# Layer norm over the heads of a decoder block: its mean folded into two weights, its Newton steps moved from VectorE to GpSimd

## The chip, the cores and the metric

The kernel runs on one core of a Trainium2 chip. Its time is the device time of one execution, in microseconds (us), given as the median of several runs. Five engines work beside each other, each through its own queue, strictly in the order of that queue: TensorE (PE), ScalarE (ACT), VectorE (DVE), GpSimd (POOL) and SyncE (SP, which only issues transfers). They wait for each other by semaphores.

## The reference, cut to what matters

Two decoder layers run over x and a context of 32 x 64 x 128 each. The first layer is: causal attention with 16 heads of 8, a cross attention, and a feed-forward part with fp4 rounding. Only the cross attention is touched. Its queries and keys are projected, and then each head (8 numbers) of each token is normed:

```python
def _layernorm(x, g, b):
    mu = jnp.mean(x, axis=-1, keepdims=True)
    var = jnp.mean(jnp.square(x - mu), axis=-1, keepdims=True)
    return (x - mu) * jax.lax.rsqrt(var + LN_EPS) * g + b
# q = _layernorm(heads of x @ Wq), k = _layernorm(heads of ctx @ Wk), LN_EPS = 1e-5
```

Then follow scores, softmax, the mix of values, a projection, the sum with x, and a norm over all 128 numbers of a token.

## The kernel before

The 2048 tokens are cut into four chunks of 512 (4 tiles of 128). Two chunks, the streams s0 and s1, run at a time, so the body of the loop runs twice; these are pass 1 and pass 2. Each engine's program for one stream is a Python generator (`network(h)`), and `weave` interleaves the programs of s0 and s1 by the numbers in `ORDER`, turn by turn. What stands in an engine's queue is thus fixed when the kernel is built: an instruction whose input is late holds up all behind it, of the other stream too.

A stream's way through the first attention and into the second, with the names used below:

- `attention_tiles` works on tiles t = 0 to 3 of a stream: scores (PE L494), row maximum and subtraction (DVE L1114, L1119), exponential (ACT L899), transposes (PE L479) and their copies (ACT L879), mix (PE L540), division (DVE L1129, L1132, into `heads`), transpose (PE L524), its copy (ACT L890), projection (PE L506), sum with x (DVE L1084), mean and variance (DVE L1087, L1090), reciprocal root of the variance (POOL L1512 adds epsilon, POOL L1515 raises to -0.5, into `rs`), and the normed x (DVE L1095).
- The keys of the second attention are projected early, in PSUM bank 1 (PE L551 from `cT`). This is norm j = 1, "k" below. The queries (PE L551 from `xT`, bank 0) come when x is there, with the values behind them (PE L465). This is norm j = 0, "q".
- `heads_norm` on DVE norms them, 64 heads of 8 per partition: `centre` sums each head (L1184), divides by 8 (L1187) and subtracts (L1190); ACT squares the result (`square_heads`, L863); `invert` sums the squares (L1195), adds epsilon (L1198), makes a first guess of the reciprocal root by an integer shift and subtraction (L1202, L1205) and begins three Newton steps of three instructions each (L1170, L1173, L1176); `scale` ends them and multiplies (L1214).
- PE turns the result (`turn_heads`, L564), ACT applies gain and bias (L869) and spreads queries (L850) or keys (L857, four instructions) for the scores. `take_values` (ACT L838) copies the values, and ACT L828 copies the turned x.
- `residual` (POOL L1531) adds a bias row to x for the sum of the second attention.

Ahead of the loop PE turns the fp4 weights (L809, L811), ACT copies them (L1027 to L1029), and SP issues all loads.

## Time and profile before

| | |
|---|---|
| median of 3 runs | 902.3 us (901.3 to 907.78) |
| span of the profiled execution | 900.6 us |
| busy: PE / DVE / ACT / POOL | 716.8 / 561.2 / 364.6 / 97.5 us |
| instructions: PE / DVE / ACT / POOL | 5017 / 1492 / 592 / 226 |
| chain that ended last: PE / DVE / ACT / POOL | 64% / 19% / 10% / 1% of the span |

The span goes from the first to the last instruction of one profiled execution; the median is of other executions, and lies 1.7 us above it. The profile counts one fp32 matmul as two records (the 128x128 projection L506 appears 96 times for 48 projections).

### The profile page before, as it was taken

How to read it: one execution, taken by the hardware profiler on the slowest of the kernel's cores; microseconds unless marked ns; L12 is line 12 of the kernel's file. 1: busy time of each engine (PE TensorE's matmuls, PEld its weight loads, DVE VectorE, ACT ScalarE, POOL GpSimd, SP SyncE). 2: the span in 40 equal slices, each digit the busy share in tenths (PEclk: the TensorE clock that was granted, in tenths of full speed). 3: DMA queues.
4: the chain of work that ended last, by engine and by line, in shares of the span. 5: the costliest groups of instructions: out<-in, count | busy, mean ns of one | idle time of the engine just before them, and what ended most of it. 6: DMA issues, size and time to landing. Idle time of an engine off the chain costs nothing.

```text
span 900.6 us, 13187 instructions
## 1 busy us (share of the span) xinstructions
PE 716.8 (80%) x5017; PEld 459.7 (51%) x5017; DVE 561.2 (62%) x1492; ACT 364.6 (40%) x592; POOL 97.5 (11%) x226
## 2 busy tenths in 40 slices
PE   0899559765788798899968974895668969979995
PEld 0557436543454365466634663473535525746664
DVE  6366746789576455655555575569976745546455
ACT  0744444312566443322236434441238554432221
POOL 2001200102102101000010020011110130100002
PEclk9999879968699899999989997796879999989998
DMA  9000100000000000000000000000000000000000
GB/s 314 3 1 2 47 1 1 1 1 0 1 1 1 0 1 1 1 1 1 1 26 1 2 1 1 1 1 1 0 1 0 1 1 1 1 1 1 1 1 24
DMA packets 8867, 10.11 MB, mean 11 GB/s; under 512 B 1240, under 2 KB 7776, under 8 KB 8288
## 3 DMA queue, kind: packets, MB, share of 16 engines
q1 hardware_dynamic: 8800, 9.22, 3.1%
q8 instruction: 42, 0.69, 0.3%
q14 instruction: 25, 0.20, 0.1%
HBM read 8.17 MB, written 1.05 MB: 10 GB/s over the span
## 4 chain that ended last, share of the span: by engine, by line
PE 64%; DVE 19%; ACT 10%; issue 4%; POOL 1%; DMA 0%; another core or an unknown queue 0%; SPq 0%; POOLq 0%; DVEq 0%
PE ps L778 13%; PE ps L494 12%; PE ps L540 8%; PE ps L769 6%; PE ps L479 6%; ACT s_q L850 3%; PE ps L488 2%; PE ps L465 2%; PE ps L723 2%; PE ps L728 2%; DVE s_work L1060 1%; PE ps L551 1%; DVE s_work L1070 1%; DVE s_work L1073 1%; PE ps L506 1%
## 5 line engine op out<-in xcount | busy, mean ns | idle before, releaser
L494 PE MATMUL ps<-s_k,s_q 128*64 128x256 f32 x768 | 118.9, 443 | 13.8 <-ACT s_q L850 13.8
L1114 DVE TENSOR_REDUCE s_row_max<-ps 128x16 f32<-128x1024 f32 x48 | 58.8, 1224 | 102.4 <-PE ps L494 102.1
L1011 ACT ACTIVATE s_k<-ps,eb 128x512 f32<-128x512 f32 x64 | 44.0, 687 | 134.7 <-PE ps L778 134.7
L1512 POOL TENSOR_TENSOR s_rs<-s_mv,eps 128x1 f32<-128x1 f32 x96 | 19.0, 200 | 690.0 <-DVE s_mv L1090 510.1
L879 ACT ACTIVATE s_pT<-ps 128x512 f32<-128x512 f32 x96 | 56.5, 596 | 82.5 <-PE ps L479 82.0
L494 PEld LDWEIGHTS ps<-s_k,s_q 128*64 128x64 f32 x768 | 54.3, 155 | 58.5 <-issue 31.6
L1447 DVE SCALAR_TENSOR_TENSOR s_pT<-ps,eb,s_k 128x512 f32<-128x512 f32 x64 | 47.9, 749 | 57.0 <-ACT s_k L1011 53.7
L540 PE MATMUL ps<-s_v,s_pT 128*64 128x108 f32 x1536 | 81.4, 260 | 1.7 <-ACT s_headsT L890 1.7
L540 PEld LDWEIGHTS ps<-s_v,s_pT 128*64 128x64 f32 x1536 | 72.8, 137 | 11.3 <-issue 11.0
L769 PEld LDWEIGHTS ps<-wo,s_pT 128*128 128x128 f32 x512 | 61.7, 192 | 17.7 <-issue 12.4
L778 PE MATMUL ps<-s_xT,wg 128*128 128x512 f32 x128 | 68.1, 614 | 1.5 <-DVE s_pT L1447 1.1
L778 PE MATMUL ps<-s_xT,wu 128*128 128x512 f32 x128 | 68.9, 621 | 0.0
L479 PE MATMUL ps<-tabs,s_probs 128*128 128x128 f32 x384 | 60.9, 285 | 8.8 <-ACT s_probs L899 7.9
L769 PE MATMUL ps<-wo,s_pT 128*128 128x128 f32 x512 | 63.0, 276 | 3.1 <-DVE s_pT L1447 3.1
L899 ACT ACTIVATE s_probs<-s_probs 128x1024 f32<-128x1024 f32 x48 | 50.4, 1054 | 30.9 <-DVE s_probs L1119 30.8
L1119 DVE TENSOR_TENSOR s_probs<-ps,s_row_max 128x1024 f32<-128x1024 f32 x48 | 58.7, 1223 | 1.5
L479 PEld LDWEIGHTS ps<-tabs,s_probs 128*128 128x128 f32 x384 | 41.9, 142 | 30.1 <-issue 17.6
L1515 POOL TENSOR_TENSOR s_rs<-s_rs,minus_half 128x1 f32<-128x1 f32 x96 | 52.7, 550 | 7.2
L1439 DVE SCALAR_TENSOR_TENSOR s_k<-ps,s_ew,s_k 128x128 f32<-128x128 f32 x128 | 36.0, 343 | 13.2 <-PE ps L769 13.2
L488 PE MATMUL ps<-cmask,identb 128*128 128x512 bf16 x64 | 26.2, 409 | 19.2 <-ACT s_q L850 14.4
L778 PEld LDWEIGHTS ps<-s_xT,wu 128*128 128x128 f32 x128 | 25.1, 196 | 31.6 <-issue 31.6
L1129 DVE RECIPROCAL s_rden<-ps 128x16 f32<-128x16 f32 x48 | 12.1, 251 | 37.1 <-PE ps L540 37.1
(221 smaller groups left out, 1154.2 us busy)
## 6 DMA issues: line engine op xcount, KB each, us to landing
mats<-in_mats SPq DMA_DIRECT2D x1, 1216.0 KB, 9.0
s_cin<-in_ctx SPq DMA_DIRECT2D x4, 256.0 KB, 4.1
s_xin<-in_x SPq DMA_DIRECT2D x4, 256.0 KB, 4.5
wg<-in_wg SPq DMA_DIRECT2D x1, 1024.0 KB
wu<-in_wu SPq DMA_DIRECT2D x1, 1024.0 KB
wo<-in_wo SPq DMA_DIRECT2D x1, 1024.0 KB
out_x<-s_x SPq DMA_DIRECT2D x4, 256.0 KB, 2.4
fc<-in_fc SPq DMA_DIRECT2D x2, 256.0 KB
```

The costliest lines, as they stand in the source:

```text
L479: ins = pe.transpose(h.ps[:, 2, tile(j)], h.probs[:, t % 2, 8 * part + 2 * j:8 * part + 2 * j + 2, :] .rearrange("p h k -> p (h k)"), ident)
L488: pe.matmul(h.ps[:, bank, :].rearrange("p (h k) -> p h k", k=S), identb[:, :], cmask[:, :].rearrange("p (o k) -> p o k", o=1).to_broadcast ...
L494: ins = pe.matmul(h.ps[S * b:S * b + S, bank, 256 * (g % 2):256 * (g % 2) + 256], h.q4[:, g, S * sq:S * sq + S], h.k4[:, sq, :, :].rearran ...
L540: ins = pe.matmul(h.ps[S * b:S * b + S, 3, 18 * j:18 * j + WINDOW * (DK + 1)], h.pT[:, t % 2, j, S * b:S * b + S], h.v2_all[:, v0:v0 + WIN ...
L769: ins = pe.matmul(h.ps[:, 2, tile(t)], h.ehid[:, e % 2, m, tile(t)], wo[:, 2 * e + m, :], start=m == 0, stop=m == 1)
L778: ins = pe.matmul(h.ps[:, k, 0:TOK], w[:, n // 2, P * (n % 2):P * (n % 2) + P], h.xT[:, :], start=True, stop=True)
L879: act.activation(h.pT[:, t % 2, 4 * part:4 * part + 4, :].rearrange("p j q -> p (j q)"), h.ps[:, 2, :], ACT.Copy).then_inc(h.pT_here, 1)
L899: act.activation(h.probs[:, u % 2, :, :], h.probs[:, u % 2, :, :], ACT.Exp).then_inc(h.exped, 1)
L1114: dve.tensor_reduce(h.row_max[:, t % 2, :], s3, AX, ALU.max).then_inc(h.max_here, 1)
L1119: dve.tensor_tensor(h.probs[:, t % 2, :, :], s3, h.row_max[:, t % 2, :].rearrange("p (h o) -> p h o", o=1).to_broadcast([P, H, S]), ALU.su ...
L1447: dve.scalar_tensor_tensor(h.ehid[:, (n // 2) % 2, n % 2, :], h.ps[:, 1, 0:TOK], eb[:, 1, n:n + 1], h.esg[:, n % 2, :], ALU.add, ALU.mult) ...
L1515: pool.tensor_tensor(h.rs[:, t % 2:t % 2 + 1], h.rs[:, t % 2:t % 2 + 1], minus_half[:, 0:1], ALU.pow).then_inc(h.rstd_here, 1)
```

## The change

- The mean of each head is a linear function of the projected row, so subtracting it is a matrix: identity minus the block matrix with 1/8 inside each head. A new table `centre` holds it, and ahead of the loop PE multiplies the two weights `a1_q` and `a1_k` by it and ACT writes the products over them. `centre()` with its three DVE instructions is gone, and ACT squares what PE left in PSUM.
- The squares are summed on DVE as before and epsilon is added, scaled by 8 (L1184 after the change); the factor 8 under the root is put back in the last multiplication.
- The Newton steps run on POOL, in a new function `rsqrt_heads`: three steps of four instructions on 64 numbers per partition. They stand in POOL's program between the norms of the first attention (`norms(h, 0)`) and `residual`.
- The last multiplication (L1196 after the change) reads the projection from PSUM and waits for POOL.
- The numbers of `ORDER` for DVE and POOL are new.

```diff
-HEADS_NORM = 17
+HEADS_NORM, RSQRT = 5, 12
     "pool": (
-        1, 1, 4, 1, 2, 2, 2, 1, 1, 5, 4, 2, 4, 6, 6, 2, 2, 2, 2, 6, 2, 2, 9, 9, 4, 2, 4, 6, 8, 8,),
+        1, 1, 6, 2, 14, 18, 13, 13, 4, 2, 4, 6, 6, 2, 2, 2, 2, 6, 2, 2, 9, 9, 4, 2, 4, 6, 8, 8,),
...
+            pe.wait_ge(mats_here, 16)
+            for k, w in enumerate(CENTRED):
+                ins = pe.matmul(ps[:, 4, tile(k)], mat(w), tab("centre"), start=True, stop=True)
+            ins.then_inc(centred, 1)
+            pe.wait_ge(centred_here, 1)
...
             def square_heads(h, j):
                 yield
-                act.wait_ge(h.hln, HEADS_NORM * (1 - j) + 3)
-                act.activation(h.qk2[j], h.qk[j], ACT.Square).then_inc(h.squared, 1)
+                act.wait_ge(h.k_proj if j else h.q_proj, 2)
+                act.activation(h.qk2[j], h.ps[:, j, 0:TOK].rearrange("p (h d) -> p h d", d=DK), ACT.Square).then_inc(h.squared, 1)
...
+            act.wait_ge(centred, 1)
+            for k, w in enumerate(CENTRED):
+                ins = act.activation(mat(w), ps[:, 4, tile(k)], ACT.Copy)
+            ins.then_inc(centred_here, 1)
...
-                centre, invert, scale = heads_norm(h, 1)
-                yield from attention_tiles(h, 0, 0, h.xin, {1: centre, 2: invert, 3: scale})
+                sum_squares, scale = heads_norm(h, 1)
+                yield from attention_tiles(h, 0, 0, h.xin, {2: sum_squares, 4: scale})
...
-                def centre(h):
...
-                    dve.tensor_tensor(h.qk[j], src, over(h.qks), ALU.subtract).then_inc(h.hln, 1)
-                def invert(h):
+                def sum_squares(h):
                     yield
                     dve.wait_ge(h.squared, 2 - j)
                     dve.tensor_reduce(h.qkv, h.qk2[j], AX, ALU.add).then_inc(h.hln, 1)
                     yield
-                    dve.wait_ge(h.hln, c + 4)
-                    dve.tensor_scalar(h.qkv, h.qkv, 1.0 / DK, EPS, ALU.mult, ALU.add).then_inc(h.hln, 1)
+                    dve.wait_ge(h.hln, c + 1)
+                    dve.tensor_scalar(h.qkv, h.qkv, DK * EPS, None, ALU.add).then_inc(h.hln, 1)
...
-                    yield from newton(c + 7)
-                    yield from newton(c + 10)
                 def scale(h):
-                    yield from newton(c + 13)
                     yield
-                    dve.wait_ge(h.hln, c + 16)
-                    dve.tensor_tensor(h.qk[j], h.qk[j], over(h.qky), ALU.mult).then_inc(h.hln, 1)
+                    dve.wait_ge(h.rsqrt, RSQRT * (2 - j))
+                    dve.scalar_tensor_tensor(h.qk[j], src, float(DK) ** 0.5, h.qky.rearrange("p (h o) -> p h o", o=1)
+                                             .to_broadcast([P, G, DK]), ALU.mult, ALU.mult).then_inc(h.hln, 1)
...
+            def rsqrt_heads(h, j):
+                c = RSQRT * (1 - j)
+                for k in range(3):
+                    yield
+                    if k == 0:
+                        pool.wait_ge(h.hln, HEADS_NORM * (1 - j) + 4)
+                    else:
+                        pool.wait_ge(h.rsqrt, c + 4 * k)
+                    pool.tensor_tensor(h.qkt, h.qky, h.qky, ALU.mult).then_inc(h.rsqrt, 1)
+                    yield
+                    pool.wait_ge(h.rsqrt, c + 4 * k + 1)
+                    pool.tensor_tensor(h.qkt, h.qkt, h.qkv, ALU.mult).then_inc(h.rsqrt, 1)
+                    yield
+                    pool.wait_ge(h.rsqrt, c + 4 * k + 2)
+                    pool.tensor_scalar(h.qkt, h.qkt, -0.5, 1.5, ALU.mult, ALU.add).then_inc(h.rsqrt, 1)
+                    yield
+                    pool.wait_ge(h.rsqrt, c + 4 * k + 3)
+                    pool.tensor_tensor(h.qky, h.qkt, h.qky, ALU.mult).then_inc(h.rsqrt, 1)
...
             def network(h):
                 yield from norms(h, 0)
+                yield from rsqrt_heads(h, 1)
+                yield from rsqrt_heads(h, 0)
                 yield from residual(h, 1, bp)
```

Two places of the queues show what moved. The first is DVE's queue where the k norm of s0 ends. `s0_work` is the small array of the norm, `s0_probs` holds the normed heads, `mv` is mean and variance. Before:

```order
L1090 BN_AGGR s0_mv<-s0_st 128x2 [waits s0_stat]
L1095 TENSOR_SCALAR s0_x<-s0_r,s0_mv,s0_rs 128x128 [waits s0_rstd_here]
L1170 TENSOR_TENSOR s0_work<-s0_work 128x64 [waits s0_hln]
L1095 TENSOR_SCALAR s1_x<-s1_r,s1_mv,s1_rs 128x128 [waits s1_rstd_here]
L1173 SCALAR_TENSOR_TENSOR s0_work<-s0_work 128x64 [waits s0_hln]
L1176 SCALAR_TENSOR_TENSOR s0_work<-s0_work 128x64 [waits s0_hln]
L1214 TENSOR_TENSOR s0_probs<-s0_probs,s0_work 128x512 [waits s0_hln]
L1129 RECIPROCAL s1_rden<-ps 128x16 [waits s1_mixed]
```

In the six rows before these stand two more Newton steps; the last multiplication followed at once. After:

```order
L1105 BN_AGGR s0_mv<-s0_st 128x2 [waits s0_stat]
L1110 TENSOR_SCALAR s0_x<-s0_r,s0_mv,s0_rs 128x128 [waits s0_rstd_here]
L1110 TENSOR_SCALAR s1_x<-s1_r,s1_mv,s1_rs 128x128 [waits s1_rstd_here]
L1110 TENSOR_SCALAR s0_x<-s0_r,s0_mv,s0_rs 128x128 [waits s0_rstd_here]
L1144 RECIPROCAL s1_rden<-ps 128x16 [waits s1_mixed]
L1196 SCALAR_TENSOR_TENSOR s0_probs<-ps,s0_work 128x512 [waits s0_rsqrt]
L1147 TENSOR_TENSOR s1_heads<-ps,s1_rden 128x128 [waits s1_den_here]
```

The Newton steps are gone from DVE, and the multiplication moved behind two more rows; it waits for POOL (`s0_rsqrt`), and `s1_heads` stands behind it.

The second place is POOL's queue at the same point. Before, `rs` of s0's tile 3 and of s1's tile 1 came as a pair:

```order
L1512 TENSOR_TENSOR s1_rs<-s1_mv,eps 128x1 [waits s1_mean_here]
L1512 TENSOR_TENSOR s0_rs<-s0_mv,eps 128x1 [waits s0_mean_here]
L1515 TENSOR_TENSOR s0_rs<-s0_rs,minus_half 128x1 [waits s0_eps_added]
L1515 TENSOR_TENSOR s1_rs<-s1_rs,minus_half 128x1 [waits s1_eps_added]
L1531 TENSOR_TENSOR s0_resid<-s0_x,bp 128x512 [waits s0_x_new]
```

After (the four Newton rows L1520 to L1529 stand three times in a row; then come the three `rs` that s1 still needs, and then s1's Newton steps):

```order
L1496 TENSOR_TENSOR s0_rs<-s0_mv,eps 128x1 [waits s0_mean_here]
L1499 TENSOR_TENSOR s0_rs<-s0_rs,minus_half 128x1 [waits s0_eps_added]
L1520 TENSOR_TENSOR s0_work<-s0_work 128x64 [waits s0_hln]
L1523 TENSOR_TENSOR s0_work<-s0_work 128x64 [waits s0_rsqrt]
L1526 TENSOR_SCALAR s0_work<-s0_work 128x64 [waits s0_rsqrt]
L1529 TENSOR_TENSOR s0_work<-s0_work 128x64 [waits s0_rsqrt]
```

The Newton steps of s0's keys stand behind `rs` of s0's last tile, so they wait for that tile's mean too.

## Rows read from the trace of the kernel before

**Rows 1.** The page, busy us of each engine (share of the span) xinstructions.

```profile
PE 716.8 (80%) x5017; PEld 459.7 (51%) x5017; DVE 561.2 (62%) x1492; ACT 364.6 (40%) x592; POOL 97.5 (11%) x226
```

**Rows 2.** Timeline of PE, pass 1: start, us, line, x, [idle before <-releaser].

```profile
89.22 0.46 PE L506 MATMUL ps<-mats,s_headsT 128*128 128x128 f32 x2 [0.52 <-DVE s_heads L1132]
...
92.88 1.16 PE L551 MATMUL ps<-mats,s_cT 128*128 128x128 f32 x8
...
99.09 1.16 PE L551 MATMUL ps<-mats,s_xT 128*128 128x128 f32 x8 [0.51 <-ACT s_xT L828]
...
111.33 1.11 PE L564 MATMUL ps<-tabs,s_probs 128*128 128x128 f32 x4 [4.01 <-DVE s_probs L1214]
115.89 3.68 PE L494 MATMUL ps<-s_k,s_q 128*64 128x256 f32 x16 [3.44 <-ACT s_q L850]
...
129.66 1.11 PE L479 MATMUL ps<-tabs,s_probs 128*128 128x128 f32 x4
```

**Rows 3.** Timeline of DVE, pass 1.

```profile
89.20 0.19 DVE L1205 TENSOR_SCALAR s_work<-s_work 128x64 int32<-128x64 int32 x1
...
91.54 0.30 DVE L1090 BATCH_NORM_AGGREGATE s_mv<-s_st 128x2 f32<-128x6 f32 x2
...
92.90 0.69 DVE L1214 TENSOR_TENSOR s_probs<-s_probs,s_work 128x512 f32<-128x512 f32 x1
...
105.77 0.69 DVE L1195 TENSOR_REDUCE s_work<-s_probs 128x64 f32<-128x512 f32 x1 [0.71 <-ACT s_probs L863]
...
107.30 1.17 DVE L1170 TENSOR_TENSOR s_work<-s_work 128x64 f32<-128x64 f32 x1
108.51 0.22 DVE L1173 SCALAR_TENSOR_TENSOR s_work<-s_work 128x64 f32<-128x64 f32 x1
...
125.30 0.69 DVE L1195 TENSOR_REDUCE s_work<-s_probs 128x64 f32<-128x512 f32 x1 [1.18 <-ACT s_probs L863]
```

**Rows 4.** Timeline of POOL, pass 1.

```profile
91.79 0.34 POOL L1512 TENSOR_TENSOR s_rs<-s_mv,eps 128x1 f32<-128x1 f32 x2 [3.56 <-DVE s_mv L1090]
...
96.96 0.20 POOL L1512 TENSOR_TENSOR s_rs<-s_mv,eps 128x1 f32<-128x1 f32 x1 [1.60 <-DVE s_mv L1090]
97.24 0.55 POOL L1515 TENSOR_TENSOR s_rs<-s_rs,minus_half 128x1 f32<-128x1 f32 x1
...
107.11 1.28 POOL L1531 TENSOR_TENSOR s_resid<-s_x,bp 128x512 f32<-128x512 f32 x1 [2.76 <-DVE s_x L1095]
```

**Rows 5.** Groups by line and shape: xcount, busy us, mean ns, idle before.

```profile
L1512 POOL TENSOR_TENSOR s_rs<-s_mv,eps 128x1 f32<-128x1 f32 x96 | 19.0, 200 | 690.0 <-DVE s_mv L1090 510.1 <-DVE s_mv L1471 179.6
L1531 POOL TENSOR_TENSOR s_resid<-s_x,bp 128x512 f32<-128x512 f32 x4 | 5.1, 1277 | 7.0 <-DVE s_x L1095 7.0
L1190 DVE TENSOR_TENSOR s_probs<-ps,s_work 128x512 f32<-128x512 f32 x8 | 5.5, 691 | 0.3
```

**Rows 6.** The chain that ended last, pass 1, in order of time.

```profile
98.56 0.49 ACT s_xT L828
99.09 1.16 PE ps L551 x8
100.25 3.45 PE ps L465 x32
```

**Rows 7.** Timelines of DVE and PE, the same places in pass 2.

```profile
537.24 2.04 PE L551 MATMUL ps<-mats,s_xT 128*128 128x128 f32 x8 [0.51 <-ACT s_xT L828]
539.20 2.69 PE L465 MATMUL ps<-mats,s_cT 128*64 128x128 f32 x32
...
562.89 0.69 DVE L1195 TENSOR_REDUCE s_work<-s_probs 128x64 f32<-128x512 f32 x1 [1.13 <-ACT s_probs L863]
...
567.93 0.69 PE L479 MATMUL ps<-tabs,s_probs 128*128 128x128 f32 x4
```

**Rows 8.** Windows: length, busy us of PE, PEld, DVE, ACT, POOL, then TensorE's granted clock.

```profile
112.00:116.00 4.00, 0.56 (x5) 0.16 (x5) 0.00 (x0) 3.28 (x5) 0.00 (x0) 0.50 0.00 0
...
584.00:588.00 4.00, 4.00 (x33) 2.33 (x29) 2.75 (x3) 1.97 (x5) 0.00 (x0) 1.00 0.00 0
```

**Rows 9.** Timeline ahead of the loop, all engines.

```profile
19.62 0.85 PE L811 MATMUL ps<-tabs,s_k 128*128 128x128 f32 x3
...
22.60 0.50 ACT L1029 ACTIVATE d_w<-ps 128x384 f32<-128x384 f32 x1
...
24.12 1.09 PE L573 MATMUL ps<-tabs,s_cin 128*128 128x128 f32 x4 [3.65 <-remote]
```

More of the change, by code:

```diff
@@ L59 @@
 MAT = {n: k for k, n in enumerate(MATS)}
-TABLES = [("ident", P), ("rope", P), ("diag", P), ("cos_q", S), ("sin_q", S), ("cos_k", S), ("sin_k", S),
+CENTRED = ["a1_q", "a1_k"]
+TABLES = [("ident", P), ("rope", P), ("diag", P), ("centre", P), ("cos_q", S), ("sin_q", S), ("cos_k", S), ("sin_k", S),
           ("head", H), ("member", GH), ("iota", EXPERTS)]
@@ L235, in stream @@
             work = sb(name + "work", [P, 7 * TOK])
-            h.qks, h.qkv, h.qky, h.qkt = (placed(work, k * TILES * H, TILES * H) for k in range(4))
+            h.qkv, h.qky, h.qkt = (placed(work, k * TILES * H, TILES * H) for k in range(3))
             h.qmax = sb(name + "qmax", [P, QW // BLOCK])
@@ L307, in stream @@
             h.squared = signal(name + "squared")
+            h.rsqrt = signal(name + "rsqrt")
             h.qk_turned = signal(name + "qk_turned")
@@ L379, in decoder @@
         fp4_w_here = sem("fp4_w_here")
+        centred = sem("centred")
+        centred_here = sem("centred_here")
         ENGINES = ("pe", "act", "dve", "pool")
@@ L1196, in invert @@
                     yield
-                    dve.wait_ge(h.hln, c + 4)
-                    dve.tensor_scalar(h.qkv, h.qkv, 1.0 / DK, EPS, ALU.mult, ALU.add).then_inc(h.hln, 1)
+                    dve.wait_ge(h.hln, c + 1)
+                    dve.tensor_scalar(h.qkv, h.qkv, DK * EPS, None, ALU.add).then_inc(h.hln, 1)
                     yield
-                    dve.wait_ge(h.hln, c + 5)
+                    dve.wait_ge(h.hln, c + 2)
                     dve.tensor_scalar(h.qkt.bitcast(I32), h.qkv.bitcast(I32), 1, None, ALU.logical_shift_right).then_inc(h.hln, 1)
                     yield
-                    dve.wait_ge(h.hln, c + 6)
+                    dve.wait_ge(h.hln, c + 3)
                     dve.tensor_scalar(h.qky.bitcast(I32), h.qkt.bitcast(I32), -1.0, float(0x5F3759DF),
                                       ALU.mult, ALU.add).then_inc(h.hln, 1)
-                    yield from newton(c + 7)
-                    yield from newton(c + 10)
                 def scale(h):
-                    yield from newton(c + 13)
                     yield
-                    dve.wait_ge(h.hln, c + 16)
-                    dve.tensor_tensor(h.qk[j], h.qk[j], over(h.qky), ALU.mult).then_inc(h.hln, 1)
-                return centre, invert, scale
+                    dve.wait_ge(h.rsqrt, RSQRT * (2 - j))
+                    dve.scalar_tensor_tensor(h.qk[j], src, float(DK) ** 0.5, h.qky.rearrange("p (h o) -> p h o", o=1)
+                                             .to_broadcast([P, G, DK]), ALU.mult, ALU.mult).then_inc(h.hln, 1)
+                return sum_squares, scale
             def cross_attention(h):
-                for part in heads_norm(h, 0):
-                    yield from part(h)
+                sum_squares, scale = heads_norm(h, 0)
+                yield from sum_squares(h)
+                yield from scale(h)
                 yield from attention_tiles(h, 1, 1, h.resid, {2: lambda h: quantize_x(h, 0)})
@@ L1576, in _tables @@
     t["diag"] = c[:, None] // DK == c[None, :] // DK
+    t["centre"] = t["ident"] - t["diag"] / DK
     angle = np.arange(S)[None, :] * (10000.0 ** (-(c % DK // 2) * (2.0 / DK)))[:, None]
@@ L1598 @@
             "a0_v": a[l0 + "Wv"].T, "a0_o": a[l0 + "Wo"].T,
-            "a1_q": a["L0_xattn_Wq"].T, "a1_k": a["L0_xattn_Wk"].T, "a1_v": a["L0_xattn_Wv"].T, "a1_o": a["L0_xattn_Wp"].T,
+            "a1_q": a["L0_xattn_Wq"], "a1_k": a["L0_xattn_Wk"], "a1_v": a["L0_xattn_Wv"].T, "a1_o": a["L0_xattn_Wp"].T,
             "in": a[l1 + "in_w"], "actp": a[l1 + "actp_w"], "q": a[l1 + "qk_w"][:, 0:P], "k": a[l1 + "qk_w"][:, P:],
```

23 lines of the change are left out of this document (removed), and 16 rows, old and new, of the table ORDER.

## The prediction, made before the changed kernel ran

> **What bounds the kernel now.** I read the page first. PE is busy for 80% of the span, DVE for 62%, POOL for 11% [rows 1]. That suggests DVE is worth relieving and that POOL has room. But shares are means over stages, and this change lives in one stage of each pass, some 50 us long, where the k and q norms of both streams run. So I went on to the timelines of this stage and ask what each engine waits for.
>
> PE's timeline shows a stage in which PE waits. It idles 4.01 us until the last multiplication of s0's q norm (DVE L1214) and 3.44 us until the spread queries (ACT L850) [rows 2]. [...] DVE is no bottleneck at these places: it stands idle until ACT has squared [rows 3]. What sets the end is one dependent chain that goes from engine to engine, and the Newton steps are a piece of it. For them the length of the piece counts, not the load of the engine that does it.
>
> **The change, part by part.** I write d for the time from one POOL Newton instruction to the next, and the reader should watch this number, since each norm has 12 of them in a row.
>
> The price of d. Two rows bound it: an addition of 1 number per partition takes 200 ns, one of 512 takes 1277 ns [rows 5]. On the line between them (2.11 ns a number) one of 64 takes 0.33 us. A dependent POOL instruction starts 0.08 us after the end of the one before (97.16 to 97.24) [rows 4]. One instruction in four is a tensor_scalar with one input; no such row stands on POOL, so I bound it by 0.20 and 0.33 and take 0.28, nearer to the line, since the number of elements is the same. The mean of a step is then (3 x 0.33 + 0.28) / 4 + 0.08 = 0.40, so d = 0.40, and 12 steps take 4.8 us. Bounds: 0.28 if 64 numbers cost no more than 1, and 0.50 if POOL's two-operand steps also meet DVE at SBUF. On DVE nine steps follow each other every 0.26 us (108.51 less 107.30 without its collision, the same in its other runs of steps), 2.3 us in all.
>
> [...]
>
> Term A, the k norm of s0. DVE's first guess (L1205) ended at 89.39, and L1214 ended at 93.59 [rows 3]. PE came to turn these heads at 94.04, when L551 for s1 was done [rows 2], so the norm was just in time. After the change POOL may start only behind `rs` of s0's tile 3. That needs the mean of the tile, which DVE gave at 91.84 [rows 3]. With the Newton steps gone from between, DVE's rows up to that mean begin at 89.72 (the projection L506 begins at 89.22 and is there at 89.68 [rows 2]) and need 1.3 us, so 91.0. Then POOL: 0.08 + 0.20 + 0.08 + 0.55 + 0.08 [rows 4], start at 92.0, end at 96.8. L1196 takes 0.05 + 0.69 (the multiplication of the same shape from PSUM [rows 5]), and PE can turn at 97.6. A = 97.6 - 94.04 = 3.6 us; in general 12d - 1.2. Queued behind the waiting L1196 on DVE is the division for s1's heads; queued behind L564 on PE are the turned x of s0 and both streams' next steps. The delay then goes on through ACT (gain, keys, square, x), PE L551 and L465 [rows 6], since each of these is next in its queue.
>
> Term B, the q norm of s0. Before, from the sum of squares (105.77) to PE's L564 (111.33) it took 5.56 us [rows 2, 3]. In it a DVE step took 1.17 instead of 0.23 us, while POOL's L1531 ran (107.11 to 108.39) [rows 3, 4]; L1531 now stands behind the Newton steps, so this 0.94 goes. After: sum 0.70, three small ones 0.67, the multiplication for s1's keys, which the queue puts between, 0.72, hand over 0.08, Newton 4.8, multiplication and hand over 0.79: 7.76. B = 2.2 us (12d - 2.6).
>
> [...]
>
> Term C, the q norm of s1. From the sum of squares (125.30) to PE being free for L564 (end of L479, 130.77) there were 5.47 us [rows 2, 3]. After: 1.39 + 0.08 + 4.8 + 0.79 = 7.06, so C = 1.6 us; in pass 2 the gap is 562.89 to 568.62 [rows 7], so C = 1.3.
>
> The k norm of s1 costs nothing by itself: POOL reaches it at about 105.4 (behind the last `rs` of s1, all shifted by A) and ends at 110.2, just as DVE comes to its multiplication between the sums of s0's q. That cover is 0.1 us thin; each 0.01 us more in d costs 0.12 more here.
>
> The removed `centre` costs 0.69 + 0.2 + 0.69 us of DVE four times a pass. It saves nothing on the path: for q the values (L465) and their copies come later than it in the queues of PE and ACT, and ACT squares behind them; for k it only lets s1's sums start earlier, and these then wait for A. The square from PSUM instead of SBUF I cost at nothing.
>
> The clock. In pass 1 L551 took 1.16 us, in pass 2 the same 2.04 at half clock; L465 took 3.50 (pass 1, from 100.18) and 2.69 (pass 2) [rows 2, 6, 7]. PE now idles 3.6 us longer ahead of them in both passes, so I expect the slower value of each twice: 0.9 + 0.8 = 1.7 us. Bounds 0 and 4.
>
> Ahead of the loop PE waited for ACT's copy, done at 23.10, and began at 24.12 [rows 9]. Two products (0.6 us with the hand over) and two copies (0.55) now lie between: 1.1 us, or 0 if the last loads were what both waited for.
>
> Sum: pass 1 3.6 + 2.2 + 1.6 = 7.4, pass 2 3.6 + 2.2 + 1.3 = 7.1, clock 1.7, start 1.1: 17.3 us. Nothing behind takes it up again in my reading: from 136 us on PE is full (for pass 2 the last window of [rows 8]), both streams come late by nearly the same, and the orders are fixed. The profiled 900.6 becomes 917.9; the median lies 1.7 above the span: **919.6 us**.
>
> **Rivals.**
>
> Cheap steps (this is the one that ends on the other side, not slower). Two independent L1512 took 0.34 together, so POOL can begin every 0.14 us [rows 4]. If dependent steps of 64 numbers come every 0.20 us, Newton takes 2.4: A = 1.2, B = -0.2, C = 0, together 2.0 for both passes, with the start 3.1: 905 us, within 1%. The 0.08 between dependent instructions and the length of L1531 speak against it. Mechanism and place: the 12 steps on POOL. It decides from about d = 0.28 down, where the sum is 7 us (909).
>
> The relief wins. If DVE's load and the collisions bound the stage between 84 and 111 us, removing 36 Newton instructions and 12 others per pass would end it earlier: 0.94 of B, and the 2.1 us of s1's `centre` in the k stage, 3 us a pass, less 1.1 at the start, so 897 us. Against it: the idle before L1195 and before L564 [rows 2, 3].
>
> Slack further on. If the later stages, where DVE rather than PE is late, take up half of the delay, 7 + 1 + 1.7 gives 912. For it: ACT and DVE queues interleave two streams, and a delay of one is partly a wait for the other anyway. Against it: both streams are late together.
>
> Collisions the other way. If POOL's steps and DVE's norms block each other, d becomes 0.50: A 4.8, B 3.4, C 2.8 and 2.5, the k norm of s1 1 us late in each pass: 24 + 3 = 27, so 929 us. Some of it is likely in A, where DVE does three norms of x beside the steps.
>
> The mean might also not be what it says: if folding it did not free ACT to square earlier at all, nothing changes in my sum, which has no gain from it.
>
> **How the numbers follow.** The forecast 0.58, cheap steps 0.14, slack further on 0.13, collisions 0.10, relief 0.05. The range leaves out the relief and the far ends: low 907, between cheap steps at 0.20 and 0.28, high 928. About 1% (9 us, 893 to 911) is what a measurement here can tell from no change. Slower by more: the forecast, nearly all of the slack case and the collisions, 0.79; within 1%: cheap steps and a bit of slack, 0.16; faster 0.05.
>
> **What would show it.** In the changed profile: POOL's rows of 128x64 near 0.33 us, every 0.40; POOL's first Newton row of s0 behind a pow at about 92, and 12 of them to 97; DVE idle before L1196 with POOL as releaser in every norm, 3 to 5 us for q; PE waiting for L1196 at s0's k norm, where it did not wait before; no DVE row of 1.17 us there; the row maximum of s0's tile 0 in the second attention some 6 to 7 us later than the end of its scores before (115.89 + 3.68), the next stage 7 to 9 us later. Wrong I would be if POOL's rows stood at 0.2, if PE's L551 of s0's queries began at 99 as before, or if the shift at 150 us were gone by 400.

## The result, and the profile after

| | before | after |
|---|---|---|
| median | 902.4 us (901.3 to 907.8) | 920.0 us (918.4 to 920.2) |
| ratio | | 1.0183, 95% interval 1.0163 to 1.0204 |
| span of the profiled execution | 900.6 us | 918.1 us |
| TensorE's mean granted clock | 0.908 | 0.889 |

The change costs 17.6 us. The page shows what it meant to do (busy us of each engine, to be held against [rows 1]):

```profile
PE 726.8 (79%) x5021; PEld 466.4 (51%) x5021; DVE 533.5 (58%) x1396; ACT 365.3 (40%) x594; POOL 126.0 (14%) x322
```

DVE is relieved of 28 us and 96 instructions, POOL has 28 us and 96 instructions more, and PE is busy for 10 us more although it has only four records more. That last number is the first hint of the clock.

What each POOL step costs, from the groups by line and shape (x, busy us, mean ns of one):

```profile
L1523 POOL TENSOR_TENSOR s_work<-s_work 128x64 f32<-128x64 f32 x24 | 7.7, 321 | 1.9
L1529 POOL TENSOR_TENSOR s_work<-s_work 128x64 f32<-128x64 f32 x24 | 7.7, 320 | 2.0
L1520 POOL TENSOR_TENSOR s_work<-s_work 128x64 f32<-128x64 f32 x24 | 7.0, 294 | 34.1 <-DVE s_work L1190 32.9
L1526 POOL TENSOR_SCALAR s_work<-s_work 128x64 f32<-128x64 f32 x24 | 5.9, 245 | 2.1
```

The line between 1 and 512 numbers [rows 5] had said 330 ns, and it was 294 to 321; the tensor_scalar was put at 280 and was 245.

The timeline of POOL, pass 1, which answers to [rows 4]:

```profile
91.95 0.20 POOL L1496 TENSOR_TENSOR s_rs<-s_mv,eps 128x1 f32<-128x1 f32 x1 [3.59 <-DVE s_mv L1105]
92.23 0.55 POOL L1499 TENSOR_TENSOR s_rs<-s_rs,minus_half 128x1 f32<-128x1 f32 x1
92.75 0.30 POOL L1520 TENSOR_TENSOR s_work<-s_work 128x64 f32<-128x64 f32 x1
93.12 0.32 POOL L1523 TENSOR_TENSOR s_work<-s_work 128x64 f32<-128x64 f32 x1
93.53 0.25 POOL L1526 TENSOR_SCALAR s_work<-s_work 128x64 f32<-128x64 f32 x1
93.86 0.32 POOL L1529 TENSOR_TENSOR s_work<-s_work 128x64 f32<-128x64 f32 x1
...
96.87 0.32 POOL L1529 TENSOR_TENSOR s_work<-s_work 128x64 f32<-128x64 f32 x1
...
109.82 0.32 POOL L1529 TENSOR_TENSOR s_work<-s_work 128x64 f32<-128x64 f32 x1
111.62 0.29 POOL L1520 TENSOR_TENSOR s_work<-s_work 128x64 f32<-128x64 f32 x1 [1.48 <-DVE s_work L1190]
```

Twelve steps run from 92.75 to 97.19, 4.44 us, so d, the time from one step to the next, is 0.37 us. They begin only behind the pow for s0's last tile (L1499), though DVE gave the first guess at 90.21.

The timeline of DVE, the same stage, which answers to [rows 3]:

```profile
90.01 0.20 DVE L1190 TENSOR_SCALAR s_work<-s_work 128x64 int32<-128x64 int32 x1
...
97.23 0.69 DVE L1196 SCALAR_TENSOR_TENSOR s_probs<-ps,s_work 128x512 f32<-128x512 f32 x1 [3.56 <-POOL s_work L1529]
...
109.70 0.69 DVE L1181 TENSOR_REDUCE s_work<-s_probs 128x64 f32<-128x512 f32 x1 [3.58 <-ACT s_probs L874]
110.53 0.68 DVE L1196 SCALAR_TENSOR_TENSOR s_probs<-ps,s_work 128x512 f32<-128x512 f32 x1
...
116.10 0.69 DVE L1196 SCALAR_TENSOR_TENSOR s_probs<-ps,s_work 128x512 f32<-128x512 f32 x1 [4.55 <-POOL s_work L1529]
...
130.90 0.69 DVE L1181 TENSOR_REDUCE s_work<-s_probs 128x64 f32<-128x512 f32 x1 [3.28 <-ACT s_probs L874]
```

DVE waits 3.56 us for s0's keys and 4.55 for its queries, with POOL as releaser. The multiplication for s1's keys at 110.53 does not wait for POOL. The timeline of PE, the same stage, which answers to [rows 2]:

```profile
93.30 1.16 PE L555 MATMUL ps<-mats,s_cT 128*128 128x128 f32 x8
97.97 0.66 PE L568 MATMUL ps<-tabs,s_probs 128*128 128x128 f32 x4 [3.52 <-DVE s_probs L1196]
...
103.22 2.08 PE L555 MATMUL ps<-mats,s_xT 128*128 128x128 f32 x8 [0.17 <-ACT s_xT L839]
105.23 2.41 PE L469 MATMUL ps<-mats,s_cT 128*64 128x128 f32 x32
...
116.85 1.12 PE L568 MATMUL ps<-tabs,s_probs 128*128 128x128 f32 x4 [4.48 <-DVE s_probs L1196]
121.41 3.68 PE L498 MATMUL ps<-s_k,s_q 128*64 128x256 f32 x16 [3.44 <-ACT s_q L861]
...
137.58 0.66 PE L568 MATMUL ps<-tabs,s_probs 128*128 128x128 f32 x4 [1.10 <-DVE s_probs L1196]
```

Before, the turn of s0's keys waited for nothing; its row in the timeline of PE of the kernel before is

```profile
93.87 0.60 PE L564 MATMUL ps<-tabs,s_probs 128*128 128x128 f32 x4
```

Now it waits 3.52 us. It begins at 97.97, which is 4.10 us later than this row, and 3.93 later than 94.04, the end of L551, from which the prediction counts. The turn of s0's queries comes 5.52 us later (116.85 against 111.33 [rows 2]), the scores as well (121.41 against 115.89), the turn of s1's queries 6.81 (137.58 against 130.77, the end of L479 [rows 2], which is the prediction's mark here).

Ahead of the loop, which answers to [rows 9] (timeline, all engines):

```profile
22.59 0.50 ACT L1040 ACTIVATE d_w<-ps 128x384 f32<-128x384 f32 x1
...
23.14 1.22 PE L822 MATMUL ps<-tabs,mats 128*128 128x128 f32 x4 [2.69 <-ACT d_w L1040]
24.39 0.45 ACT L1044 ACTIVATE mats<-ps 128x128 f32<-128x128 f32 x2 [1.31 <-PE ps L822]
...
25.20 1.09 PE L577 MATMUL ps<-tabs,s_cin 128*128 128x128 f32 x4 [0.84 <-remote]
```

The first work of the loop starts at 25.20 instead of 24.12: 1.08 us. How much of that is the price of the change is open. The kernels of experiments 7 and 9 have nothing added ahead of the loop, and their first work starts at 24.62 and 25.36.

**Where the 17 us arise.** The most useful reading is a ledger: take one instruction that every kernel runs at the same places (the row maximum on DVE, 48 of them), pair the n-th of one trace with the n-th of the other, and subtract the starts. Where the difference grows, time is lost. The heads of the columns are the starts in the kernel before; the names of the experiments are explained below.

| later than before by, us | 79.4 | 161.9 | 339.8 | 517.6 | 600.8 | 776.8 |
|---|---|---|---|---|---|---|
| after | 0.8 | 7.9 | 9.0 | 7.6 | 13.0 | 15.8 |
| fold alone | 1.2 | 2.8 | 2.7 | 2.7 | 2.7 | 2.7 |
| keys' steps first | 0.5 | 4.7 | 5.5 | 5.5 | 9.2 | 11.9 |
| two steps on POOL | 0.9 | 3.5 | 4.7 | 3.3 | 5.0 | 8.0 |
| changed, with fillers | 1.2 | 3.6 | 4.4 | 3.1 | 5.0 | 8.1 |
| fold, early square | 0.7 | -1.8 | -3.6 | -3.6 | -7.0 | -7.0 |
| changed, early square | 0.4 | 3.9 | 5.0 | 3.7 | 6.7 | 8.5 |
| fold, early, two steps on DVE | 1.0 | -3.9 | -5.6 | -5.7 | -11.0 | -9.2 |
| before, fillers at k and q | 0.5 | -0.1 | 0.0 | 2.1 | 1.5 | 3.4 |
| before, fillers at q | 1.3 | -4.4 | -5.5 | -3.4 | -8.1 | -5.5 |
| fold, early, two steps, fillers at q | 0.8 | -4.8 | -4.8 | -2.6 | -13.5 | -11.7 |

The columns 79.4 to 161.9 and 517.6 to 600.8 enclose the touched stage of pass 1 and pass 2. The changed kernel loses 7.0 us in the first and 5.5 in the second. Between them, in the rest of pass 1 and the first part of pass 2, it wins 0.3 net. From 600.8 to the end it loses another 4.4 (2.7 by 776.8; the whole span is 17.5 longer). The last loss stands where no instruction was changed.

Each row comes from one execution. Executions of one and the same kernel also differ: the kernel before took 899.5 to 905.4 us beside the experiments, and the kernel of experiment 7 took 900.1 to 907.7 us in ten executions. A difference of 1 or 2 us in one column can thus be chance; the 7.0 and 5.5 of the two stages are well above that. The windows of the piece behind 600.8, for the kernel before (length; busy us of PE, PEld, DVE, ACT, POOL with their instructions; granted clock; DMA share; GB/s):

```profile
597.60:680.00 82.40, 55.46 (x328) 37.14 (x328) 69.00 (x220) 24.36 (x44) 14.14 (x34) 0.81 0.00 1
```

and the same piece of work after:

```profile
610.70:695.70 85.00, 60.43 (x328) 39.49 (x327) 69.15 (x220) 24.38 (x44) 14.20 (x34) 0.72 0.00 1
```

The same 328 matmuls take PE 5 us more and the piece 2.6 us more, DVE, ACT and POOL take the same, and the granted clock is 0.72 instead of 0.81.

### The profile page after: what moved, and what is told of

Same layout as the page of the kernel before. It is cut to its first block, busy times and chain, and to the rows that moved or that the text cites. A ratio compares the mean times of both kernels' runs of the same rounds, so it can differ in the third digit from the quotient of the medians.

```text
span 918.1 us, 13198 instructions
## 1 busy us (share of the span) xinstructions
PE 726.8 (79%) x5021; PEld 466.4 (51%) x5021; DVE 533.5 (58%) x1396; ACT 365.3 (40%) x594; POOL 126.0 (14%) x322
## 4 chain that ended last, share of the span: by engine, by line
PE 63%; DVE 18%; ACT 10%; issue 4%; POOL 4%; DMA 0%; SPq 0%; POOLq 0%; another core or an unknown queue 0%; DVEq 0%; ACTq 0%
PE ps L782 12%; PE ps L498 11%; PE ps L544 8%; PE ps L773 6%; PE ps L483 5%; ACT s_q L861 3%; PE ps L492 2%; PE ps L469 2%; PE ps L727 2%; PE ps L732 2%; PE ps L510 1%; DVE s_work L1075 1%; ACT s_k L868 1%; DVE s_work L1085 1%; DVE s_work L1088 1%
## 5 line engine op out<-in xcount | busy, mean ns | idle before, releaser
L1499 POOL TENSOR_TENSOR s_rs<-s_rs,minus_half 128x1 f32<-128x1 f32 x96 | 53.0, 552 | 7.5
L632 PE MATMUL ps<-gu_w,s_xT 128*128 128x352 f32 x64 | 30.9, 633 | 5.8 <-DVE s_hq L1236 5.3
```

The source lines that it names most:

```text
L1499: pool.tensor_tensor(h.rs[:, t % 2:t % 2 + 1], h.rs[:, t % 2:t % 2 + 1], minus_half[:, 0:1], ALU.pow).then_inc(h.rstd_here, 1)
```

## The experiments

Ratios are to the kernel before, run again on the same chip beside each group: at 902.9 us for experiments 1 to 4, 903.3 for 5 to 8, 902.7 for 9 and 10.

### 1. The fold alone (fold_only)

The mean goes into the weights as in the change, and ACT squares from PSUM, but the Newton steps stay on DVE, where they were; the numbers of `ORDER` are those of before.

```diff
-HEADS_NORM = 17
+HEADS_NORM = 14
                 def centre(h):
...
-                    dve.tensor_tensor(h.qk[j], src, over(h.qks), ALU.subtract).then_inc(h.hln, 1)
+                    yield
+                    yield
+                    yield
```

> The mean folded into the weights, as in the change, but Newton steps, orders and POOL's program as before (the three turns of the removed centring stay empty). Theory (the steps on POOL and their place in its queue are the whole loss): before plus the 1.1 us at the start, 903 to 904, and no gain from the lighter DVE beyond 1 us. Rival (the fold costs too, by the square read from PSUM or the product of the weights): 906 or more. Rival (DVE's load bounds the stage): 898 or less.

Measured: 904.0 us, ratio 1.0014 (0.9999 to 1.0030). The time is as expected, and the fold is neutral within what these runs can tell. In the ledger it loses about 1 us at the start (see above on how sure that is) and 1.6 in pass 1's stage, and nothing after that. The 1.6 shows on PE as a low clock, not as a wait. Its timeline has

```profile
92.41 2.78 PE L543 MATMUL ps<-s_v,s_pT 128*64 128x108 f32 x32 [0.41 <-ACT s_headsT L900]
95.12 1.68 PE L554 MATMUL ps<-mats,s_cT 128*128 128x128 f32 x8
```

where the kernel before takes 1.70 us for the same mix and 1.16 us for the projection; the granted clock from 92.4 to 97.0 is 0.63, and for the same piece of the kernel before (91.2 to 94.1) it is 1.00. Removing 24 instructions from DVE bought nothing.

### 2. The keys' steps ahead of the last rs (k_first)

```diff
-                yield from norms(h, 0)
+                for t in range(TILES - 1):
+                    yield from rstd(h, 0, t)
                 yield from rsqrt_heads(h, 1)
+                yield from rstd(h, 0, TILES - 1)
                 yield from rsqrt_heads(h, 0)
...
-                yield from attention_tiles(h, 0, 0, h.xin, {2: sum_squares, 4: scale})
+                yield from attention_tiles(h, 0, 0, h.xin, {2: sum_squares, 3: scale})
```

> The changed kernel, with the Newton steps of the keys ahead of rs of each stream's last tile in POOL's queue, and DVE's last multiplication of the keys ahead of the norm of x of that tile. Theory (PE comes to the keys of s0 at 94 us and waits because the steps stand behind that tile's mean): the multiplication comes 2.4 us earlier in each pass, 915.2. Rival (only the length of the steps counts, not their place): 920, unchanged.

Measured: 914.1 us, ratio 1.0123 (1.0080 to 1.0166), 6 us better than the change. DVE's multiplication for s0's keys, timeline:

```profile
94.45 0.69 DVE L1196 SCALAR_TENSOR_TENSOR s_probs<-ps,s_work 128x512 f32<-128x512 f32 x1 [2.20 <-POOL s_work L1529]
```

It comes at 94.45 instead of 97.23, 0.3 of it from an earlier start of the stage, and PE waits 1.06 us for it instead of 3.52. So 2.5 of the 3.1 us that term A measured hang on the place in the queue: on POOL behind `rs` and the mean that `rs` waits for, where the steps can no longer hide beside PE's other work, and on DVE behind the norm of x of that tile. The run moves both and does not separate them; but DVE waits 2.20 us with POOL as releaser even now, so POOL's place is the larger part. What is left in pass 1's stage is 4.2 us by the ledger.

### 3. Two Newton steps on POOL (two_steps)

The root is less exact. RSQRT and four of POOL's numbers in `ORDER` shrink with the four missing instructions, so that the order around them stays as it was.

```diff
-HEADS_NORM, RSQRT = 5, 12
+HEADS_NORM, RSQRT = 5, 8
...
-        1, 1, 6, 2, 14, 18, 13, 13, 4, 2,
+        1, 1, 6, 2, 10, 14, 9, 9, 4, 2,
...
-                for k in range(3):
+                for k in range(2):
```

> The changed kernel with two Newton steps instead of three for each norm (8 POOL instructions in a row instead of 12; the result is a little less exact). Theory (three of a pass's four norms lie on the path, each POOL instruction at 0.37 us): 3 x 2 x 4 x 0.37 = 8.9 us less, 911. Rival (the wait for POOL is hidden behind other waits): 920, less than 2 us gained. Above 9 us only if the clock gives something back too.

Measured: 908.5 us, ratio 1.0070 (1.0047 to 1.0093). Four POOL steps fewer in each norm give back 11.6 us. Six norms of them stand on the path (A, B and C in both passes); at d = 0.37 that is 6 x 4 x 0.37 = 8.9 us. By the ledger the two stages gain 4.4 and 3.7, 8.1 together, and the rest comes behind them, in code that is the same in both kernels. So the price of the change goes with the number of dependent POOL instructions: the rival of cheap steps is out. This run says nothing about an engine being full: POOL is busy for 14% of the span.

### 4. The changed kernel with fillers on PE (warm)

PE runs bf16 products whose results nobody reads while it waits for the norms, eight or four ahead of each `turn_heads` and eight behind the queries'.

```diff
+            def fill(h, count):
+                for _ in range(count):
+                    pe.matmul(h.ps[:, 2, :].rearrange("p (h k) -> p h k", k=S), identb[:, :],
+                              cmask[:, :].rearrange("p (o k) -> p o k", o=1).to_broadcast([P, 8, S]),
+                              start=True, stop=True)
             def turn_heads(h, j):
                 yield
+                if j:
+                    pe.wait_ge(h.pT_here, 2 * TILES)
+                else:
+                    pe.wait_ge(h.v2_here, 2)
+                fill(h, 8 if j or h is streams[0] else 4)
...
+                if j == 0:
+                    fill(h, 8)
```

> The changed kernel with idle-time work for PE: 8 bf16 matmuls of 512 columns (0.2 us each at full clock) whose result nobody reads, into a free PSUM bank, ahead of each wait for the keys' and s0's queries' norm, 4 for s1's, and 8 behind each turn of the queries. Theory (the longer waits cost twice, by the clock that falls to half in them): the scores behind the norms return from 3.7 to 1.9 us and others with them, about 4 to 5 us a pass, 910 to 912. Rival (the clock costs nothing, since PE waits for others anyway): 920, or 1 to 3 us more, for what of the added work ends late.

Measured: 910.1 us, ratio 1.0081 (1.0049 to 1.0112): fillers give back 9.9 us. The scores behind s0's norm, timeline of PE:

```profile
122.24 1.95 PE L498 MATMUL ps<-s_k,s_q 128*64 128x256 f32 x16
```

They take 1.95 instead of 3.68 us, at a granted clock of 1.00 (122.2 to 124.2) instead of 0.50 (121.4 to 125.1 in the changed kernel). Eight fillers take 1.89 us at a granted clock of 1.00 (113.51 to 115.4) and 3.48 at 0.52 (118.64 to 122.1), 0.24 and 0.43 us each. By itself this doesn't say whose cost that is, the change's or one that the kernel before has as well. Experiments 7 and 9 ask that.

### 5. The fold alone, with the queries squared earlier (fold_early)

What the fold really offers is that ACT need not wait for DVE's `centre`. The change leaves the square behind the copy of the values. Here it is moved:

```diff
                 yield from take_x(h, 2, 2)
-                yield from take_values(h, 1, 2)
                 yield from square_heads(h, 0)
+                yield from take_values(h, 1, 2)
```

> The fold alone (mean in the weights, three Newton steps still on VectorE), and ScalarE now squares the queries straight behind their projection, ahead of the copy of the values. My theory: what the fold is worth is this freedom, which the change did not use. In the run with the fold alone the queries of s0 are projected by 102.9 us and their sum of squares begins at 108.5; VectorE is busy with the keys of s1 until 106.6, so 1.9 us can be had for s0 and up to 3.4 us for s1 in each pass: 4 to 7 us off its 904, so 897 to 900. Rival: the copy of the values, now behind the square, is as urgent as the square, or the wait moves to the turn of x: no gain, 904. Second rival: the whole 3.4 us twice per pass, with the clock: 890 or less.

Measured: 896.8 us, ratio 0.9934 (0.9914 to 0.9954), at the low end of what was expected (897 to 900); both rivals are out. The timeline around s0's q norm, DVE and POOL:

```profile
103.81 0.69 DVE L1218 SCALAR_TENSOR_TENSOR s_probs<-ps,s_work 128x512 f32<-128x512 f32 x1
...
104.42 0.67 DVE L1200 TENSOR_REDUCE s_work<-s_probs 128x64 f32<-128x512 f32 x1
...
105.75 1.28 POOL L1535 TENSOR_TENSOR s_resid<-s_x,bp 128x512 f32<-128x512 f32 x1 [1.95 <-DVE s_x L1109]
105.94 1.17 DVE L1184 TENSOR_TENSOR s_work<-s_work 128x64 f32<-128x64 f32 x1
```

The squares are there at 102.0, and the sum L1200 at 104.42 now waits only for its place behind the multiplication for s1's keys. The collision with POOL's L1535 is still there: 1.17 us for a DVE step that otherwise takes 0.23.

### 6. The changed kernel with the same move (after_early)

The diff is that of experiment 5, on the changed kernel.

> The changed kernel with the same move of the square of the queries. My theory: GpSimd is now the one that serializes. Its steps for the keys of s1 end at 110.1 us, so those of the queries of s0, which began at 111.6, can come only 1.4 us earlier, and VectorE takes the sum no earlier than 107.5. 1.4 to 3 us a pass: 914 to 917. Rival: the same gain as on VectorE or more (5 us and more, 913 or less), if GpSimd is free in time. Second rival: no gain, 920.

Measured: 913.0 us, ratio 1.0101 (1.0079 to 1.0123), 7 us better than the change and still 10 slower than before. That is 1 us below the range of my theory (914 to 917) and at the edge of the first rival (913 or less). The theory holds for the queries of s0, as the timeline shows:

```profile
105.59 0.68 DVE L1181 TENSOR_REDUCE s_work<-s_probs 128x64 f32<-128x512 f32 x1
...
109.71 0.69 DVE L1196 SCALAR_TENSOR_TENSOR s_probs<-ps,s_work 128x512 f32<-128x512 f32 x1 [3.21 <-POOL s_work L1529]
...
110.54 0.19 DVE L1190 TENSOR_SCALAR s_work<-s_work 128x64 int32<-128x64 int32 x1
110.81 0.29 POOL L1520 TENSOR_TENSOR s_work<-s_work 128x64 f32<-128x64 f32 x1 [1.13 <-DVE s_work L1190]
```

s0's sum is done at 106.3, but its first guess L1190 stands behind the multiplication for s1's keys, and that waits for POOL until 109.7. Then POOL itself waits 1.13 us for the guess. Each engine stands in its own queue behind the other. The sum comes 4.1 us earlier than in the changed kernel (109.70), the first Newton step only 0.8 (111.62). What the theory left out is the queries of s1:

```profile
126.92 0.69 DVE L1181 TENSOR_REDUCE s_work<-s_probs 128x64 f32<-128x512 f32 x1
133.65 0.60 PE L568 MATMUL ps<-tabs,s_probs 128*128 128x128 f32 x4
```

Their sum comes 3.98 us earlier than in the changed kernel (130.90) and their turn 3.93 us earlier (137.58). POOL has no other work there.

### 7. The kernel before with fillers (before_warm)

> The kernel before, with nothing changed but filler products on TensorE in the gaps where it waits for the norms of the queries (results unread). It tells what the slow clock costs there by itself. My theory: the scores behind each norm take 1.9 instead of 3.7 us as they did in the changed kernel with the fillers, and the gain is of the same size as there, 8 to 10 us: 893 to 895. Rival: in the kernel before the gaps are shorter and the clock is granted again soon, so the fillers cost what they save: 902. Second rival: fillers delay the work queued behind them, 906.

Measured: 906.2 us, ratio 1.0016 (0.9995 to 1.0037): no gain. My theory is out. The number is that of the second rival, but with executions from 900.1 to 907.7 us the two rivals can't be told apart by time. The timeline of PE shows the mechanism of the second, and with it a flaw of the experiment:

```profile
93.39 1.16 PE L551 MATMUL ps<-mats,s_cT 128*128 128x128 f32 x8
94.39 1.89 PE L562 MATMUL ps<-cmask,identb 128*128 128x512 bf16 x8
96.11 0.60 PE L575 MATMUL ps<-tabs,s_probs 128*128 128x128 f32 x4
```

In the kernel before there is no gap ahead of the turn of s0's keys, so the fillers push it back by 1.7 us. The result doesn't settle the clock, so experiment 9 leaves them out there.

### 8. Fold, early square, two steps on DVE, residual moved (best)

DVE does two Newton steps instead of three (a less exact root), and s0's `residual` on POOL waits for s0's q norm, so that it can't meet it.

```diff
-HEADS_NORM = 14
+HEADS_NORM = 11
...
                     yield from newton(c + 4)
-                    yield from newton(c + 7)
+                    yield
+                    yield
+                    yield
...
+                if sub == 1 and h is streams[0]:
+                    pool.wait_ge(h.hln, 2 * HEADS_NORM)
...
-        1, 1, 4, 1, 2, 2, 2, 1, 1, 5, 4, 2,
+        1, 1, 4, 1, 2, 2, 2, 5, 1, 1, 4, 2,
```

> The fold and the early square, two Newton steps instead of three on VectorE (the root is a little less exact), and the sum with the bias row on GpSimd moved behind the norm of the queries of s0 and waiting for it. My theory, from the rows of the fold alone: per pass 1.9 us from the square, 0.94 from the collision that is gone, 0.78 for each of the norms of the keys of s1, queries of s0 and of s1 that stand on the path: 4.5 to 5.2 us, so 9 to 10.5 us for both and 893 to 895. Rival: the removed pieces lie beside other waits (the turned x, the keys of s1) and half is lost: 899. If the clock gives back too: 890.

Measured: 894.9 us, ratio 0.9916 (0.9893 to 0.9940). The time is in the range, but it is only 2 us below experiment 5, whose gain is most of it, and the intervals of the two ratios overlap. By the ledger pass 1's stage is 2.4 us shorter than there, pass 2's 2.0, and 1.8 of it is lost again from 600.8 on, in unchanged code.

### 9. The kernel before with fillers only at the queries (before_fill_q)

The diff is against experiment 7.

```diff
-                if j:
-                    pe.wait_ge(h.pT_here, 2 * TILES)
-                else:
-                    pe.wait_ge(h.v2_here, 2)
-                fill(h, 8 if j or h is streams[0] else 4)
+                if j == 0:
+                    pe.wait_ge(h.v2_here, 2)
+                    fill(h, 8 if h is streams[0] else 4)
```

> The kernel before with filler products on TensorE only in the gaps of the norms of the queries, not ahead of the turn of the keys, where the kernel before has no gap and the last fillers cost 1.9 us a pass. My theory: a filler where there is no gap costs its length, and elsewhere the slow clock costs 1.7 us at each of the scores behind a norm; so this one gains where the last one did not, 3 to 6 us: 897 to 900. Rival: the kernel before loses nothing to the clock that fillers can give back, 902 to 905; then most of what fillers gave the changed kernel was the cost of the change's longer waits.

Measured: 894.7 us, ratio 0.9901 (0.9880 to 0.9922), more than my theory gave. The timeline of PE:

```profile
101.44 1.97 PE L465 MATMUL ps<-mats,s_cT 128*64 128x128 f32 x32
...
107.61 1.89 PE L562 MATMUL ps<-cmask,identb 128*128 128x512 bf16 x8
111.80 0.91 PE L573 MATMUL ps<-tabs,s_probs 128*128 128x128 f32 x4 [2.29 <-DVE s_probs L1225]
112.50 3.36 PE L562 MATMUL ps<-cmask,identb 128*128 128x512 bf16 x8
116.15 1.95 PE L494 MATMUL ps<-s_k,s_q 128*64 128x256 f32 x16 [0.29 <-ACT s_q L861]
```

The scores take 1.95 instead of 3.68 us [rows 2], at a granted clock of 1.00 (116.15 to 118.1) instead of 0.50 (115.9 to 119.6 in the kernel before). Not all of the 8 us can be put down to the fillers: the values' projection L465 takes 1.97 us here, at a granted clock of 1.00, and 3.50 at 0.53 in the kernel before, and it stands ahead of the first filler of the pass. The turn of s0's queries, which stands ahead of those scores and can't gain from them, comes 0.8 us earlier for it in pass 1 and 0.9 in pass 2, counted from the start of each stage. The two stages gain 10.4 us together by the ledger. So the kernel before too loses most of 8 us to the slow clock in these gaps (0.50 in [rows 8]), and what experiment 4 gave back is mostly not a cost of the change. Between two kernels that both have fillers, the change costs 15.4 us (910.1 less 894.7; by their ratios 1.8% or 16 us, uncertain by about 3 us, as they ran beside different runs of the kernel before, and as only the changed one has fillers at the keys, where it has a gap).

### 10. Experiment 8 with fillers at the queries (best_fill_q)

The diff is that of experiment 8 and the fillers of experiment 9 together.

> The fold with the early square, two Newton steps on VectorE and the moved sum with the bias row, and fillers in the gaps of the norms of the queries. My theory: three times a pass the scores take 1.9 instead of 3.5 us, of which one is partly hidden, so 4 to 8 us off its 894.9: 887 to 891. Rival: no gain or a loss as in the kernel before with fillers, 895 to 898.

Measured: 890.7 us, ratio 0.9856 (0.9834 to 0.9878): the fastest here, 12 us under the kernel before, with one Newton step less. With three steps and an exact root, experiment 5 (6 us) and experiment 9 (8 us) each stand by themselves; their sum was not run.

## Why the prediction was right, point by point

The forecast was 919.6 us, the time is 920.0 us. The main step is shown: the steps on POOL lie on the dependent chain, and the price goes with their number (experiment 3), while the fold itself is neutral (experiment 1). But the agreement to 0.4 us is luck: the stages cost 3.7 us less than forecast, and code behind them, put at nothing, cost 4.1 us more.

| term | predicted, us | measured, us |
|---|---|---|
| start | 1.1 | 1.1 at PE's first product, 0.8 by the ledger |
| pass 1: A, B, C | 3.6, 2.2, 1.6 | 3.1, 1.6, 1.3 |
| pass 2: A, B, C | 3.6, 2.2, 1.3 | 3.1, 1.6, 1.0 |
| pass 1, projections at the slow clock | 0.9 | -0.2 |
| pass 2, projections at the slow clock | 0.8 | 0.7 |
| both stages, by the ledger | 16.2 | 12.5 |
| behind the stages | 0 | 4.1 |

- **d.** The step was put at 0.40 us and took 0.37. The choice of the line between 1 and 512 numbers was right, and the POOL steps did not collide with DVE, so the upper bound of 0.50, an estimate of the author for a collision that no run shows, fell: the two-input steps took 0.294 to 0.323 us. With 0.37 the formulas give A = 3.2, B = 1.8, C = 1.2: most of the error of these terms is d.
- **The start** has the right number from two wrong halves. The products and the copies took 1.75 us (23.09 to 24.84) and not 1.15, and the wait of 1.02 us ahead of the first product, which was taken as fixed, shrank to 0.36. The prediction's own condition, "0 if the last loads were what both waited for", may hold in part: with no added work the same place comes at 24.12, 24.62 and 25.36 in three kernels.
- **A** measured: the turn of s0's keys comes 3.93 us later, 0.84 of it from the start. Its cause, the place behind `rs`, is confirmed by experiment 2, with the reserve said there. The start is the 1.08 of PE; at the row maxima of pass 1 it is 0.84. In pass 2 the same turn comes at 542.89 instead of 532.18, and the stage begins 7.6 us late by the ledger, so A is 3.1 again.
- **B** measured: 5.52 less 3.93 is 1.6. From the sum of squares to PE's turn it takes 7.15 us (109.70 to 116.85) instead of 5.56. The collision that was taken as removed is gone: no DVE step of 1.17 us stands there. L1535 now runs at 116.02 beside L1196, which takes its usual 0.69. Beside L1535 a DVE step with both inputs in SBUF took 1.17 us instead of 0.23 in experiment 5, and L1196, with one input in PSUM, was not lengthened here; whether the place of the inputs is what decides was not run. In pass 2 the same stretch takes 7.15 us against 5.57, so B is 1.6 there too.
- **C** measured: 6.81 less 5.52 is 1.3. In pass 2, from the sum of squares to PE's turn, it is 6.68 us (575.93 to 582.61) against 5.73, so 1.0. **The keys of s1** cost nothing, as said; POOL ended at 110.14 and DVE came at 110.53, so the cover was 0.4 us, and not 0.1.
- **The clock** is where the prediction was wrong in place, and mis-sized. It was sought at L551 and L465. In pass 1 the pair took 2.08 + 2.41 = 4.49 us, no more than before (1.16 + 3.50), at granted clocks of 0.50 and 0.80 against 1.00 and 0.53. The clock's part of pass 1 stands further on: from the scores behind s1's norm to the end of the next tile's scores PE needs 6.97 us (141.68 to 148.65), where the kernel before needs 5.90 (134.89 to 140.79), with the granted clock at 0.61 and 0.74. That 1.1 us is what A, B and C leave over of the 7.0 of the ledger. In pass 2 it is as said, by the timeline of PE against [rows 7]:

```profile
548.44 2.07 PE L555 MATMUL ps<-mats,s_xT 128*128 128x128 f32 x8 [0.17 <-ACT s_xT L839]
550.45 3.35 PE L469 MATMUL ps<-mats,s_cT 128*64 128x128 f32 x32
```

  5.42 against 4.73 us, at granted clocks of 0.50 and 0.57 against 0.52 and 0.72. What was missed is the 4.1 us outside the stages. "Nothing behind takes it up again" was right, but the code behind can also add. Is this the price of being late? The ledger says no: between 600.8 and 776.8 the kernels that come *earlier* than before by 8, 11 or 13 us (experiments 9, 8 and 10) lose 1.8 to 2.6 us too, and the fold alone and experiment 5, later by 2.7 and earlier by 7.0, lose nothing. Between 339.8 and 517.6 some kernels gain 1.4, some lose 2.1. Behind 776.8 two kernels (experiments 2 and 3) gain 1.9, and three, the changed one among them, lose 1.7. The windows above show that the lost time goes with a lower granted clock, for one case. Whether it is the shift that decides, or the execution, stays open: only one execution of each kernel was traced, and executions of one kernel differ by as much. Such a part of 2 to 4 us can't be predicted from the trace of before, and would belong in the range.
- **The rivals.** Cheap steps: out, by d. The relief: out, by experiment 1; without the POOL steps the kernel is at 904.0. Slack further on: out, nothing but 1.4 us is given back. Collisions: out, DVE's norms of x beside the Newton steps take 0.35 us against 0.32 to 0.34 before; DVE stands idle for most of the steps, so there was little to collide with. That the fold could "free ACT to square earlier" was noted as a mere aside, with no gain in the sum; experiments 5 and 6 show that it was the one thing in the change that these runs found of worth, 7 us if ACT's program is put in the other order.
- **The signs.** POOL's first Newton step behind a pow at about 92, twelve of them to 97, and no row of 1.17 us came as said. Two did not: the row maximum of s0's tile 0 comes 5.5 us later (125.13 against 119.62) and not 6 to 7, and DVE waits for POOL in three norms of a pass and not in every one, as it does not for the keys of s1.

## What to carry to other kernels

Moving dependent small steps from a busy engine to an idle one costs the difference in time per step, times the steps, for each time that they stand on the chain, and the idle engine's queue adds what stands ahead of them; busy shares say nothing about either. Count the steps anew as well: here a norm went from 9 steps of 0.26 us to 12 of 0.37, 2.1 us more, and about half of that comes from the fourth instruction that each Newton step needs in this form. POOL raises 128x1 numbers to -0.5 in one instruction of 0.55 us [rows 4]; whether one such instruction on 128x64 numbers could stand in for the twelve was not run. When a change removes a dependency, look for the instruction that could now go earlier, and move it: here that was worth 7 us, with the relief worth nothing. Test an idea about the clock on the kernel before as well, since a gain that both kernels can have is not the change's cost.

## What the runs showed of the hardware

- A dependent POOL instruction of 128x64 fp32 took 0.29 to 0.32 us with two inputs, 0.245 with one, and the next began 0.08 us after it: 0.37 us a step (the changed kernel), where DVE's chain had 0.26 (the kernel before).
- With eight bf16 products of 128x512 in the gap of PE ahead of them, the fp32 scores took 1.95 instead of 3.68 us, at a granted clock of 1.00 instead of 0.50, in the kernel before and after alike (experiments 4 and 9). Where there was no gap, the products delayed what followed by 1.7 us (experiment 7).
- A DVE tensor_tensor of 128x64 with two inputs in SBUF took 1.17 us beside a POOL instruction of 128x512, and 0.23 otherwise (experiment 5).
- Code that nobody touched differed in length by -1.9 to +3.1 us from one column of the ledger to the next. In the piece that was looked at, DVE, ACT and POOL were busy for the same time, and the granted clock was 0.72 instead of 0.81. Executions of one kernel differ too, by up to 7.6 us (experiment 7).
